# GpSimd's gathers as a register-driven loop of 23 turns instead of written-out code, in a graph attention layer on one core

## The reference

```python
xp = (x @ W).reshape(n, 4, 64)
e = leaky_relu(a_src[src] + a_dst[dst], 0.2)
alpha = softmax of e over the edges of one dst
gat = relu(segment_sum(alpha[:, :, None] * xp[src], dst))
x = x + gat + mix(norm(x))
x = x + experts(norm(x))      # 8 experts, three 256x256 layers
```

## Time and profile before

| what | value |
|---|---|
| median of 3 runs | 4522.06 us (4509.46 to 4523.47) |
| the profiled execution, its own time | 4533.09 us |
| its span in the profile | 4531.3 us |
| mean granted TensorE clock | 0.777 of full speed |
| busy share of the span | PE 68%, DVE 50%, ACT 34%, GpSimd (POOL) 33% |

### The profile page before, as it was taken

The page is one execution under the profiler, slowest core; times in us unless marked ns, Lnnn a source line. Parts: engine busy times, 40 slices in busy tenths (PEclk is TensorE's granted clock), DMA queues, the critical chain, the costliest instruction groups (busy, mean ns, idle before and its releaser), DMA issues. The chain is left out here.

```text
span 4531.3 us, 61905 instructions
## 1 busy us (share of the span) xinstructions
PE 3060.9 (68%) x18597; PEld 2300.8 (51%) x18597; DVE 2272.4 (50%) x6619; ACT 1531.8 (34%) x4022; POOL 1500.6 (33%) x1629
## 2 busy tenths in 40 slices
PE   6345655465555556656665555555657999999999
PEld 5334544344444455545544444444545666666665
DVE  5244454444544544444444454544547666666653
ACT  2133333233333333333333333333334333333333
POOL 2445444444444444443444443444440000000000
PEclk8667676667666777676777776776768999999999
DMA  7323222222222233222333222222222110101100
GB/s 251 84 77 84 75 76 77 74 76 77 69 75 67 76 85 87 80 79 72 83 85 85 72 72 66 71 75 71 75 71 91 46 33 25 33 9 33 31 11 9
DMA packets 203310, 315.96 MB, mean 70 GB/s; under 512 B 77409, under 2 KB 137442, under 8 KB 202850
## 3 DMA queue, kind: packets, MB, share of 16 engines
q0 software_dynamic: 75360, 212.42, 17.6%
q1 hardware_dynamic: 119874, 92.43, 6.8%
q10 hardware_dynamic: 7744, 7.15, 0.5%
HBM read 279.51 MB, written 26.86 MB: 68 GB/s over the span
## 5 line engine op out<-in xcount | busy, mean ns | idle before, releaser
L770 POOL DMA_INDIRECT xg<-edge_table,idx x1564 | 1484.6, 949 | 1831.6 <-ACT y L922 777.4
L1070 PE MATMUL ps_y<-y,hotw 128*128 128x260 f32 x3512 | 1038.8, 462 | 810.8 <-DVE y L1302 627.9
L1070 PEld LDWEIGHTS ps_y<-y,hotw 128*128 128x128 f32 x3512 | 796.8, 234 | 1029.4 <-ACT hotw L981 600.9
L1444 DVE TENSOR_TENSOR acc<-acc,ps_y 128x260 f32 x439 | 186.7, 425 | 1273.9 <-remote 981.3
L981 ACT CAST hotw<-hot 128x512 f32<-128x512 bf16 x439 | 265.8, 620 | 1025.1 <-remote 665.3
L922 ACT ACTIVATE y<-xg,w 128x65 f32 x1756 | 464.0, 337 | 9.1 <-issue 1.9
L872 ACT COPY hot_t<-ps_o 128x1024 bf16<-128x1024 bf16 x220 | 212.8, 1014 | 660.9 <-remote 507.1
L1302 DVE TENSOR_TENSOR y<-xg,ps_v 128x780 f32<-128x780 f32 x439 | 417.0, 960 | 8.6
L1820 DVE SCALAR_TENSOR_TENSOR xg<-ps_ye,wts,xg 128x256 f32<-128x256 f32 x392 | 189.8, 484 | 400.2 <-PE ps_ye L1610 400.0
L1610 PE MATMUL ps_ye<-wo,xg 128*128 128x256 f32 x1568 | 352.8, 382 | 0.7 <-DVE xg L1820 0.7
L1600 PE MATMUL ps_h<-xg,w 128*128 128x448 f32 x896 | 348.2, 542 | 1.0 <-issue 0.5
(11 more groups left out here) (288 smaller groups left out, 3416.0 us busy)
## 6 DMA issues: line engine op xcount, KB each, us to landing
xg<-edge_table,idx POOLq DMA_INDIRECT x1564
mix_rows<-kk SPq DMA_DIRECT2D x49, 257.0 KB
xg<-mix_rows SPq DMA_DIRECT2D x7, 1799.0 KB, 7.8
xb<-in_xt SPq DMA_DIRECT2D x50, 128.0 KB
xnk<-in_x SPq DMA_DIRECT2D x50, 128.0 KB
x<-in_x SPq DMA_DIRECT2D x7, 896.0 KB, 13.3
xt<-in_xt SPq DMA_DIRECT2D x7, 896.0 KB, 14.6
xb<-in_xt SPq DMA_DIRECT2D x24, 256.0 KB
```

The costliest lines, as they stand in the source:

```text
L770: pool.indirect_dma_start(xg[:, q * OCT + u, j, :], None, dr["table"], bass.IndirectOffsetOnAxis(ap=idx[q][:, c:c + 1], axis=0)).then_inc( ...
L1070: mm = pe.matmul(ps_y[v % 2][:, 0:RW], hotw[v % 2][:, j, :], y[v % 2][:, j, :], start=(j == 0), stop=(j == CH - 1))
```

## The change

The first octet stays written out. Octets 1 to 46 become a loop of LOOP = 49 // 2 - 1 = 23 turns with two octets in its body, so that the buffer number `1 - k` and the ring slots stay constants. Octets 47 and 48 are written out behind it. In the loop the octet number is `i * 2 + (k + 1)`, an expression of the loop's register. From it come the count of the wait on `idx_d`, the address of the load from `K.freed`, the counts of the 8 waits on `got` in each octet, and the slice of `K.ix` that is staged. The gathers themselves keep constant destinations and constant index addresses.

```diff
         OCT = 8
+        LOOP = NGP // OCT // 2 - 1
...
-                def octet(q, o, first, more):
+                def octet(q, o, groups, first, more):
 
                     pool.wait_ge(idx_d, ONE + o + 1)
                     settle(pool, settled)
-                    for u in range(min(OCT, NG - o * OCT)):
+                    for u in range(groups):
...
                 stage(0, slice(0, OCT * CH))
-                for o in range(NGP // OCT):
-                    octet(o % 2, o, o == 0, o + 1 < NGP // OCT)
+                octet(0, 0, OCT, True, True)
+                with pool.Fori(0, LOOP) as i:
+                    for k in range(2):
+                        octet(1 - k, i * 2 + (k + 1), OCT, False, True)
+                for o in range(2 * LOOP + 1, NGP // OCT):
+                    octet(o % 2, o, min(OCT, NG - o * OCT), False, o + 1 < NGP // OCT)
```

## The result

The changed kernel takes 4537.98 us (median of 14 runs, 4521.29 to 4550.14) against 4522.88 us for the kernel before (14 runs, 4489.11 to 4531.52): a ratio of 1.0041, interval 1.0022 to 1.0059. It is slower by 15 us. The ratios in this document are not quotients of the two medians shown (here 1.0033); the two ways differ by up to 0.002. Two executions, one of the kernel before at 7005 us and one of e12 at 5188 us, were in a slower state, and no ratio uses them. The time lies inside the range of the prediction, but the forecast of no change does not hold: 0.41%, or 15 us of the medians, is beyond the 0.3% (14 us) that was named as the bound.

What follows compares the result with a forecast made beforehand. The prediction took the kernel as bound by hand-overs between PE, DVE and ACT, held up in GpSimd's gather bursts. Its terms summed 0 + 0 + 0 + 0, leaving 4533.09 us profiled, 4522 us against the median; range 4474 to 4562 us.

Steps and rivals of the forecast that it cites:

- the forecast of no change: Whole kernel: all terms 0, so 4533.09 us profiled stay, or 4522 us against the median; chance 0.42.
- What bounds the kernel: Attention stage: hand-overs between PE, DVE and ACT are held up during GpSimd's gather bursts; GpSimd itself has idle time.
- the holds at the add: DVE at L1444 waits for PE's products, released by "remote" a few us after gathers stop: 981 us in 112 waits.
- Gathers and staging: GpSimd: 1564 gathers with 0.30 us between them and one 0.22 us index copy per octet, unchanged: 0 us.
- The branch: End of each of GpSimd's 23 loop turns: 53 ns each, 1.2 us, covered; direct cost 0.
- The unknown, a fetch in each turn: Code fetch at GpSimd's branch: 0 to 159 us of GpSimd time, 53 us with one fetch a turn.
- Both rivals that rest on pauses at the branch: Fetch pauses on GpSimd either release late signals, 4484 us, chance 0.31, or lengthen bursts, 4548 us, chance 0.17.
- The faster one: Branch pauses of about 2.3 us inside bursts let held signals through: gain 25 to 51 us, 4484 us; chance 0.31.
- Instructions saved: Second instruction queue: removing written-out octets saves some 20 packets among queues busy 0.1% of the time: 0 us.
- Register work: 14 register operations per octet on GpSimd hide under gathers: taken as 0, far end 95 us of gather time.
- the register work shows: Rival: register operations come between gathers and lengthen bursts; up to 47 us, middle 24 us slower; chance 0.10.
- the last sentence of the prediction: The forecast is wrong if late signals react to changes in GpSimd's rhythm too small for the profile rows.

Runs made afterwards that it cites:

- e12: The changed kernel with 144 semaphore increments ahead of GpSimd's first gather, shifting its loop's code: 4483.36 us, 1.0042 of the kernel before.
- e7: The kernel before with every second group's landing wait moved from ahead of its fourth gather to ahead of its first: 4043.00 us, 0.9043.
- e8: The kernel before with every group's landing wait moved ahead of its first gather: 4101.31 us, 0.9162.
- e10: The kernel before with every group's landing wait ahead of its second gather: 3652.92 us, 0.8195.
- e16: The kernel before with every group's landing wait ahead of its third gather, on the chip where the kernel before took 3180.23 us: 3232.94 us, 1.0169.
- e17: The kernel before with every group's landing wait ahead of its third gather, on a chip with late signals: 4524.44 us, 0.9987.
- e4: The changed kernel's loop as 11 turns over four octets instead of 23 over two: 4528.03 us, 1.0007 of the kernel before.
- e3: The kernel before with one fused register instruction of three additions, otherwise unused, ahead of each of the 1564 gathers: 4550.11 us, 1.0049.
- e1: The change with its 23 turns written out, turn number in a register, no branch: 4529.05 us, 1.0009 of the kernel before; repeated, 4477.61 us, 1.0026.
- e6: The kernel before with a small loop of two turns ahead of each of the 391 groups' landing waits: 4456.83 us, 0.9968.
- e2: The kernel before with 144 semaphore increments ahead of GpSimd's first gather, shifting its gather code: 4521.39 us, 0.9995.
- e14: The changed kernel with every group's landing wait ahead of its second gather, where the kernel before took 3180.23 us: 3652.74 us, 1.1484.
- e15: The change written out without branch, turn in a register, landing wait ahead of each group's second gather; kernel before 3180.23 us: 3655.42 us, 1.1484.
- e9: The changed kernel with every second group's landing wait ahead of its first gather: 4050.62 us, 0.9082 of the kernel before.
- e18: The changed kernel, unaltered, timed again in the fifth follow-up comparison: 4543.68 us, 1.0033 of the kernel before.
- e13: The kernel before with every group's landing wait ahead of its second gather, on the chip where the kernel before took 3180.23 us: 3648.86 us, 1.1479.
- run 23: Not a run's label: "run" is a verb here; the changed kernel's loop body of 140 instructions is executed 23 times; that kernel took 4537.98 us, 1.0041.

## Why the prediction was wrong

**What bounds the kernel: right.** The chain of hand-overs held up in GpSimd's bursts was read from the earlier trace rows. e7, e8 and e10 move one wait and so make pauses; the holds at the add fall to 277, 5 and 4 us, and 9.6, 8.4 and 18.0% of the time go with them. Those rows showed the right cause; they didn't show that over 800 us hung on it (4467.43 less 3652.92, whatever the clock gave of it), or that it is not there on every chip: e16 and e17 are one kernel, at 3232.94 and 4524.44 us.

**Gathers and staging, 0 us: right.** 1564 gathers at 0.30 us, as the timeline of the changed kernel shows.

**The branch: right.** The stated 1.2 us are 23 x 50 ns = 1.15 us, covered. The unknown, a fetch in each turn, did not occur: 162 packets after, 164 with a body of twice the length, and no gap at the branch. The rule cited there from the Trainium skill (Runtime: NRT & Kernel Launch, Instruction fetch mechanics) speaks of targets outside the window. The body is 140 instructions, not over 144, and would fit in two blocks of the 256 that the Trainium skill states there and in two packets of 124 alike. e4's 278 fit in two such blocks but not in two such packets, and the trace agrees with the Trainium skill's figure: 164 packets, nothing fetched again. What a target outside the window costs, no run shows. Both rivals that rest on pauses at the branch fell. The faster one's mechanism, a pause that ends a hold, is real all the same (e7, e8, e10).

**Instructions saved, 0 us: right as far as shown.** 19 packets fewer, near the 20 named, and no gain.

**Register work, "I take 0": the step that failed.** The argument was that the 0.50 us in front of every second group already hide in a gather, so 0.15 more would. They do hide: the gaps didn't change. But hidden in the gathers' pace is not free in the kernel. e3, with nothing but such instructions, lost 22 us (13 to 31); the 530 of e1 lost 0.0009 and 0.0026 in two comparisons, on the mean 8 us, and 530 x 14 ns = 7.4 us. So the term that was put at 0 measures some 8 us, between 2 and 14 us by the two intervals together. The rival "the register work shows" had the right sign, but not the way (gaps over 0.30 us) and not the size (24 us in the middle). What held is the last sentence of the prediction, in part: the time reacts to changes too small for those rows, whether by way of the holds or not.

**The whole.** The changed kernel came out at 1.0041, 1.0030, 1.0042 (e12) and 1.0033 in four comparisons: mean 1.0037, 16.5 us of 4,525. Each interval lies above 1, so the loss is shown. That the time fell inside the stated range says little for the prediction: it was as wide as it was for a gain of 25 to 51 us and for losses by pauses and gaps, and none of these came. The register work explains some 8 us of the loss. The rest, 0.0019 of the time, is barely more than the two means can tell apart (each single interval reaches 0.002 to either side), and no experiment assigns it: 782 branches made nothing slower in e6, though there pauses may hide a cost; nothing is fetched again (162 packets), the shift of the code did nothing that shows (e2, e12), and a loop with 11 turns cost 1.0007 (up to 1.0023). It stays open, whether there is a second cost at all or only scatter between builds.

**Also open** is the way from a hidden 14 ns to the kernel's time. That it runs by way of the holds is argued, not shown. e14 and e15, where without holds the loop and the registers cost 3.9 and 6.6 us, do not exclude the full 8 us. In e9, with 277 us of holds in its counterpart e7, the loss was 0.2% by the medians and 0.4% by the ratios. And the sum of the holds at the add does not follow the time: 937.5 us in e3 and 886.0 in e12, both slower than the kernel before with its 981.3. What makes the holds, on three chips and not on a fourth, no run here tells.

## What to carry to other kernels

An engine with 67% of idle time is not free. Ask what its activity does to the others before you cost an edit on it at nothing: here breaking its dense bursts of gathers gained over 800 us, and 1,573 hidden instructions cost 22 us. The way to price such a thing is to multiply it until it stands clear of the scatter (1,573 instructions, not 554) and to repeat the comparison, since in two profiles of one kernel the sums of remote waits lay 45 us apart, three times the whole effect (e18 less the profile after). And where long waits are put down to "remote", try a pause in the busy stream, at more than one place, and on more than one chip: the best version here was 18% faster on one and 15% slower on another, where the holds did not occur.

## What the runs showed of the hardware

- While gathers start every 1.25 us, TensorE's signals reach DVE and ACT late: 981 us in 112 waits of DVE, the longest 19.4 us. Pauses of 1.4 us on the mean per four gathers nearly end it at DVE's add (3.5 us left in e10); gaps of 0.30 us don't (976.8 us in e17).
- On one chip of the comparisons it didn't occur: no such wait in e13 and e16, and the kernel before took 3180 us there, against 4467 to 4529 us. The trace of e16 keeps 24,553 of the gathers' 25,024 semaphore records, that of the kernel before 4,206.
- PE's granted clock while gathers ran was 0.71 in the kernel before, 0.79 in e10 and 0.83 in e16; one of its matrix products at L1070 took 462, 412 and 408 ns on the mean.
- A loop on GpSimd: 50 ns for the branch, 32 to 147 ns for register instructions, and bodies of 140 and of 278 instructions run 23 and 11 times without being fetched again (162 and 164 packets against 181).
- Under gathers a register instruction can take 707 ns where the median is 86 (e3), and a branch 1,409 where it is 45 (e6). In e3 the gaps under 1 us between gathers moved from 0.309 to 0.310 us.
